# Turning the experts' token tiles as 16-bit halves: two bf16 transposes for one f32 transpose

## The reference

```python
x = x + xattn(_layernorm(x), ctx_1024, ctx_1024)
x = x + ffn(_layernorm(x), ...)

# ffn, on the 8192 rows xt
_, idx = jax.lax.top_k(logits + beta, K)                 # K = 2 of E = 8
probs = jax.nn.sigmoid(jnp.take_along_axis(logits, idx, axis=-1))
g = jnp.einsum('bh,ehm->bem', xt, gate_proj_w)
u = jnp.einsum('bh,ehm->bem', xt, up_proj_w)
h = jax.nn.silu(g) * u
eo = jnp.einsum('bem,emh->beh', h, down_proj_w)
combined = jnp.einsum('beh,be->bh', eo, c)               # c holds the two probs
```

## Time and profile before

| | |
|---|---|
| median of 3 executions | 396.43 us (396.29 to 396.60) |
| the profiled execution: time, span of its records | 396.57 us, 394.9 us |
| TensorE (PE) busy, matmuls | 379.7 us (96%), 3321 |
| weight loads (PEld) busy | 318.3 us (81%) |
| VectorE (DVE), ScalarE (ACT), GpSimd (POOL) busy | 294.4 us (75%), 236.2 us (60%), 251.0 us (64%) |
| mean granted TensorE clock | 0.996 of full speed |

### The profile page before, as it was taken

The page is one execution under the profiler, slowest core; times in us unless marked ns, Lnnn a source line. Parts: engine busy times, 40 slices in busy tenths (PEclk is TensorE's granted clock), DMA queues, the critical chain, the costliest instruction groups (busy, mean ns, idle before and its releaser), DMA issues.

```text
span 394.9 us, 11090 instructions
## 1 busy us (share of the span) xinstructions
PE 379.7 (96%) x3321; PEld 318.3 (81%) x3321; DVE 294.4 (75%) x1308; ACT 236.2 (60%) x558; POOL 251.0 (64%) x275
## 2 busy tenths in 40 slices
PE   8979999999999999899999999999999999999993
PEld 3445666666666665689999999999999999999993
DVE  4988989999998896687966666667677666666662
ACT  2689898798888863355566565652211565656540
POOL 6636888888877787338787788886100045645464
PEclk9999999999999999999999999999999999999998
DMA  7953464896442112247556775554332113332223
GB/s 239 354 165 103 141 210 136 253 280 199 136 149 83 64 62 77 70 120 143 104 86 91 87 100 77 72 81 59 59 74 55 36 21 54 45 48 23 26 22 27
DMA packets 43049, 41.78 MB, mean 106 GB/s; under 512 B 5688, under 2 KB 31808, under 8 KB 42992
## 3 DMA queue, kind: packets, MB, share of 16 engines
q1 hardware_dynamic: 30864, 30.69, 26.8%
q0 software_dynamic: 12128, 10.40, 19.1%
HBM read 24.17 MB, written 16.90 MB: 104 GB/s over the span
## 4 chain that ended last, share of the span: by engine, by line
PE 57%; POOL 1%; issue 1%; DVE 1%; ACT 0%; POOLq 0%; DVEq 0%
PE gu_pair L1609 35%; PE bank L1633 17%; PE bank L1575 2%; PE bank L1548 1%; POOL out L529 1%; PE bank L1536 0%; PE gu_pair L1822 0%; POOL sorted_rows L478 0%; PE bank L1527 0%; DVE acc L1008 0%; PE gu_pair L1560 0%; DVE hid L1002 0%; ACT tile_T L727 0%; DVE t_out L1211 0%; DVE t_part L1205 0%
## 5 line engine op out<-in xcount | busy, mean ns | idle before, releaser
L529 POOL DMA_INDIRECT out<-t_out,tile_in x64 | 100.2, 1565 | 85.0 <-DVE t_out L1211 70.6
L1609 PE MATMUL gu_pair<-tile_T,W_slot 128*128 128x128 f32 x1024 | 124.8, 275 | 0.5 <-ACT tile_T L727 0.5
L1609 PEld LDWEIGHTS gu_pair<-tile_T,W_slot 128*128 128x128 f32 x1024 | 119.5, 192 | 0.7 <-issue 0.7
L756 ACT ACTIVATE t_silu<-gu_pair 128x512 f32<-128x512 f32 (+1 forms) x78 | 46.4, 594 | 101.8 <-PE gu_pair L1609 94.8
L1171 DVE SCALAR_TENSOR_TENSOR t_hid<-t_silu,gu_pair 128x512 f32<-128x512 f32 (+1 forms) x78 | 53.1, 680 | 48.4 <-PE gu_pair L1609 47.2
L1633 PE MATMUL bank<-W_down,t_hid 128*128 (+1 forms) x620 | 82.3, 276 | 0.1
L478 POOL DMA_INDIRECT sorted_rows<-rows,slot x64 | 63.4, 990 | 20.5 <-issue 20.0
L1633 PEld LDWEIGHTS bank<-W_down,t_hid 128*128 128x128 f32 x620 | 75.4, 192 | 0.7 <-issue 0.7
L746 ACT ACTIVATE W_slot<-W 128x512 f32 x128 | 73.2, 622 | 3.9 <-DVE slot_pair L1062 2.0
L489 POOL DMA_INDIRECT left_in<-sorted_rows,left_index x27 | 26.1, 967 | 16.8 <-DVE left_index L1089 8.9
L441 POOL TENSOR_TENSOR rstd<-var_eps,minus_half 128x8 f32<-128x8 f32 (+1 forms) x19 | 27.9, 1470 | 10.9 <-DVE var_eps L902 10.5
(11 more groups left out here) (158 smaller groups left out, 543.5 us busy)
## 6 DMA issues: line engine op xcount, KB each, us to landing
tile_in<-sorted_rows SPq DMA_DIRECT2D x91, 66.5 KB, 2.0
x_sb<-x SPq DMA_DIRECT2D x16, 256.0 KB, 4.4
c_T<-ctx_cols SPq DMA_DIRECT2D x16, 256.0 KB, 3.1
c_sb<-ctx SPq DMA_DIRECT2D x16, 256.0 KB, 4.6
out<-acc SPq DMA_DIRECT2D x16, 256.0 KB
sorted_rows<-padding SPq DMA_DIRECT2D x1, 2128.0 KB, 12.7
sorted_rows<-left_in SPq DMA_DIRECT2D x27, 66.5 KB, 2.4
sorted_rows<-rows,slot POOLq DMA_INDIRECT x64, 3.1
```

Source lines behind the costliest of these rows:

```text
L529: e.indirect_dma_start(out_flat, bass.IndirectOffsetOnAxis(ap=tile_in[:, tiles_of(i)[0] % NR, ID:ID + 1].bitcast(I32), axis=0), t_out[:, q ...
L756: e.activation(t_silu[:, 0:n * M], gate_up_pair[i % 2][0][:, 0:n * M], ACT.Silu).then_inc(s_t_silu, 1)
L1609: r = e.matmul(bank[:, c:c + P], w, tile_T[:, i % TX, tile], start=True, stop=True, skip_group_check=True)
```

## The change

From the third step on, `transpose_tile` views each tile's 128 f32 values per token as 256 16-bit values. It turns the 128 low and the 128 high halves in a transpose each, with the bf16 identity `ident_bf`, into adjoining 128-column bf16 parts of the same PSUM bytes. The stationary operand is then every second 16-bit value of a row. VectorE's copy reads the parts as 16-bit integers and writes each value beside its other half. The first two steps stay as they were. Matmuls, waits, buffers and their order are unchanged.

```diff
+U16 = mybir.dt.uint16
...
+        tile_halves = [b.bitcast(BF16) for b in tile_pair]
...
                 if i >= TX:
                     e.wait_ge(s_t_up, i - TX + 1)
-                e.tensor_copy(tile_T[:, i % TX, 0:n].rearrange("p h n -> p (h n)"), tile_pair[i % 2][:, 0:n * P]).then_inc(s_tile_T, 1)
+                e.tensor_copy(tile_T[:, i % TX, 0:n].bitcast(U16).rearrange("p h (n c) -> p h c n", c=2),
+                              tile_halves[i % 2][:, 0:n * 2 * P].bitcast(U16).rearrange("p (h c n) -> p h c n", h=n, c=2)
+                              ).then_inc(s_tile_T, 1)
...
                 for h, n in enumerate(tiles):
-                    r = e.transpose(tile_pair[i % 2][:, h * P:(h + 1) * P], tile_in[:, n % NR, 0:D], ident[:])
+                    if i < 2:
+                        r = e.transpose(tile_pair[i][:, 0:P], tile_in[:, n % NR, 0:D], ident[:])
+                        continue
+
+                    halves = tile_in[:, n % NR, 0:D].bitcast(BF16).rearrange("p (d c) -> p d c", c=2)
+                    for c in range(2):
+                        r = e.transpose(tile_halves[i % 2][:, (2 * h + c) * P:(2 * h + c + 1) * P], halves[:, :, c], ident_bf[:])
                 r.then_inc(s_t_transposed, 1)
```

## The result

| | before | after |
|---|---|---|
| median of 4 executions | 396.51 us | 402.97 us (402.48 to 403.55) |
| ratio | | 1.0162, 95% interval 1.0145 to 1.0180 |
| the profiled execution: time, span | 396.57, 394.9 us | 402.48, 400.7 us |

The change makes the kernel slower by 6.5 us in the medians, 5.9 between the two profiled executions. The profiled one is the fastest of the four.

A forecast was written before the change was run, and what follows sets the result against it. TensorE's unbroken row of instructions was taken to bound the kernel; 4.3 us of exposed loads plus 0.26 behind VectorE's copies gave 4.6, so 401.0 us against the median of 396.43, range 399.9 to 403.5 with rival (3).

The forecast's parts named there:

- rival (3): VectorE's copy much dearer, 0.7 us or more for one tile: 402.1 and over, up to 403.5; chance 0.06.
- The exposed load: First down matmul's f32 weight load outlasts the bf16 transpose hiding it: 0.056 or 0.058 us a pair, +4.3 us.
- TensorE still without pauses: Expected sign in the profile after: TensorE never idles, while one-tile periods are 2.85 us and two-tile ones 2.96.
- the stretch of the clears: VectorE almost without pause from about 182.4 to 199 us; dearer copies there delay a down matmul, +0.26 us.
- The unseen price: Weight load of a tile's halves, every second element: between nothing and 0.11 us, taken as hidden.
- Rival (2): Load of every second element takes 0.11 us, as an f32 load: +9.8 us, 406.2; chance 0.08.
- Rival (1): Down weights load early enough to be hidden after all; only VectorE's 0.54 us stays: 397.0; chance 0.09.
- Rival (4): Faster than before, needing an f32 transposition that costs more than 0.11 us where it stands; chance 0.02.
- The copy: VectorE's copy of 256 16-bit elements per tile: +0.135 us for one tile, twice that for two.
- In the long stage it costs nothing: Dearer copies are covered there: VectorE busy 13.0 of 20 us, 1.8 of each 2.79 us pair.
- One stretch has no such cover: Only from about 182.4 to 199 us, after `extra_table` and with three clears, do dearer copies delay TensorE.
- the term of 0.26: Delay added near 196.56: four copies 0.54 plus chain start 0.22, less TensorE's own 0.50 us.

The follow-up runs named there:

- the halves apart: Changed kernel with its copy on ScalarE, high halves transposed behind tile_down, ahead of the next gate-up: 404.74 us, ratio 1.0204.

## Why the prediction was right, and where it was not

**The direction and the main term.** The forecast was slower by 4.6 us, 401.0, in a range of 399.9 to 403.5; measured were 402.97, inside the range. That is partly luck: the forecast alone, widened, reached only to 402.4, and the rest was there for rival (3), a copy of 0.7 us or more for one tile, which measured 0.44. The exposed load was taken as 0.056 us a pair and 0.058 with two tiles, 4.3 in all; it measured just that, 4.27. Its signs came as written: 178 bf16 transposes 0.06 us apart, first down matmuls of 0.33, periods of 2.85 and 2.96. The sign "TensorE still without pauses" did not come.

The stage's 6.05 us are accounted for: 4.27 for the exposed loads, 1.70 for VectorE in the two-tile pairs, 0.06 in the stretch of the clears (6.03 together).

**The unseen price.** The load of every second element was bounded by nothing and 0.11 us, and taken low. It lasts 98 ns, near the 96 of a load of adjoining elements, and costs nothing here: the transposes start 0.056 us apart. The Trainium skill, page "TensorE: Matmul & The Clock Gate", section "Weight-path perf modes — Fast Weight Load (FWL) and DoubleRow", has the fast load for 128 weights that are not f32, packed or strided. This trace agrees. Rival (2) falls: it needed transposes 0.11 us apart, and they are 0.06. The 81 ns for a load and a matmul that the Trainium skill, page "TensorE: Matmul & The Clock Gate", section "Back-to-back issue gap", gives don't show either: the trace has 0.056.

**Rival (1)**, hidden down weights, falls by the 0.33 us matmul and by the halves apart. Rival (4) falls with the result.

**The copy.** Taken were +0.135 us for one tile, +0.27 for two. The rows grew by 0.157 and 0.31. But a row's duration is not what it costs in a row of them: from the start of a copy to that of the next instruction it is 0.13 us more for one tile (0.33 at 193.36 after, 0.20 at 193.13 before) and 0.29 more for two (303.48 to 304.10, for 0.33). So the forecast was near.

**The step that failed** is the sentence "In the long stage it costs nothing", with its neighbour "One stretch has no such cover". There are two such stretches. The cover was read from 340 to 360 us, one-tile pairs, and taken for the whole stage. In the two-tile pairs VectorE has another list: two `extra_sum` rows, and for every second pair a load of registers (line 1186 before), in which it stands still for 1.04 us. That this is the register load is inferred: it is the only thing in VectorE's list there, the time is the same in both kernels, and nothing that the profile shows ended it in the kernel before. No run varied it. The timeline of VectorE in the kernel before, which the prediction did not read:

```profile
301.36 0.68 DVE L1171 SCALAR_TENSOR_TENSOR t_hid<-t_silu,gu_pair 128x512 f32<-128x512 f32 x1
301.96 0.42 DVE L1121 COPY tile_T<-bank 128x256 f32<-128x256 f32 x1
302.29 0.34 DVE L1156 SCALAR_TENSOR_TENSOR t_match<-tile_in,extra_e 128x2 f32<-128x2 f32 x2
...
303.87 0.35 DVE L1196 SCALAR_TENSOR_TENSOR extra_sum<-bank,t_weight,extra_sum 128x128 f32 x1 [1.04 <-issue]
...
304.70 0.68 DVE L1171 SCALAR_TENSOR_TENSOR t_hid<-t_silu,gu_pair 128x512 f32<-128x512 f32 x1
...
307.05 0.68 DVE L1171 SCALAR_TENSOR_TENSOR t_hid<-t_silu,gu_pair 128x512 f32<-128x512 f32 x1
```

From one `t_hid` to the next but one, with one register load between (the 1.04 us ahead of 303.87), it is 307.05 - 301.36 = 5.69 us, while TensorE takes 2 x 2.90 = 5.80. VectorE never waits for another engine there, so 5.69 is its own pace. The cover was 0.05 us a pair, not 0.98. After (the bracket names TensorE, whose down matmuls had ended at 307.73, 0.57 us before the wait did; the length of 1.04 is that of before):

```profile
302.88 0.68 DVE L1177 SCALAR_TENSOR_TENSOR t_hid<-t_silu,gu_pair 128x512 f32<-128x512 f32 x1
303.48 0.73 DVE L1125 COPY tile_T<-bank 128x512 uint16<-128x512 uint16 x1
304.10 0.33 DVE L1162 SCALAR_TENSOR_TENSOR t_match<-tile_in,extra_e 128x2 f32<-128x2 f32 x2
...
305.51 0.68 DVE L1177 SCALAR_TENSOR_TENSOR t_hid<-t_silu,gu_pair 128x512 f32<-128x512 f32 x1
306.11 0.73 DVE L1125 COPY tile_T<-bank 128x512 uint16<-128x512 uint16 x1
...
308.30 0.35 DVE L1202 SCALAR_TENSOR_TENSOR extra_sum<-bank,t_weight,extra_sum 128x128 f32 x1 [1.04 <-PE bank L1645]
...
309.13 0.68 DVE L1177 SCALAR_TENSOR_TENSOR t_hid<-t_silu,gu_pair 128x512 f32<-128x512 f32 x1
```

Two pairs take 309.13 - 302.88 = 6.25 us, TensorE's 2 x 2.955 = 5.91. VectorE falls behind by 0.17 us a pair, 2.2 us over 13 pairs; about 0.5 of it would be the lead it had, and TensorE loses the rest, 44.82 - 43.12 = 1.70 us. Busy time hid this: VectorE's rows fill only part of such a loop, as the time of a register load counts as idle. With 1.7 added, the forecast would have been 4.6 + 1.7 = 6.3, against 6.05 in the stage and 6.5 in the medians. Rival (3) had named VectorE, but as a copy of 0.7 us or more for one tile; its sign, pauses of TensorE behind VectorE, came about with copies of 0.44 and 0.73 us, since two-tile pairs had only 0.05 us to spare.

**The stretch of the clears.** Expected was the down matmul near 196.56 later by 0.7 to 0.8. Counted from the first gate-up matmul it is at 196.56 - 169.98 = 26.58 before and at 196.92 - 169.72 = 27.20 after, 0.62 later, of which TensorE alone makes 0.50. So the term of 0.26 measured 0.12. The chain's start moved by 0.22, as forecast, but the four copies added 0.40 and not 0.54: the first of them, at 182.96, only 0.04, since what stands behind it started 0.41 us later before and 0.45 after, and the others 0.13 each. Over the whole stage it is 0.06, as the down matmuls behind the pause take 1.15 us in both kernels: the two pauses there cost 0.56 us for 0.50.

## What to carry to other kernels

A cheaper matmul isn't cheaper for what stands behind it: a weight load that ran exactly as long as the matmul in front becomes visible when that matmul is halved, once for each place where a long load follows a short matmul. Whether an engine has slack is to be read in each part of a loop with its own instruction list, from start to start of the same instruction over a whole cycle, register loads and waits included, not from busy time in one part.

## What the runs showed of the hardware that was not expected

The weight load of 128 bf16 values at a step of two elements lasts 98 ns, for 96 with adjoining ones. ScalarE copies 256 16-bit values per partition out of PSUM, with a strided write, in 446 ns, VectorE in 441: two engines with nearly one price. A pause of TensorE costs more than the idle time that the profile shows: 0.44 us for 0.23, 1.17 for 0.95. Most of that is the rest of the modelled row in front. A further 0.05 is that the eight down matmuls behind a pause take 1.16 us, those at 306.62 without one 1.11. Why is not tested; the weight load waits for `t_hid` too and can't run ahead.
